# Seven block products instead of eight in the down-projections of six units of an MLP

## The reference, cut to what matters

```python
attn_out = jnp.einsum('btT,bTd->btd', attn, v) @ Wp + bp
cms_out = jax.nn.gelu(attn_out @ cW1 + cb1, approximate=False) @ cW2 + cb2
cms_out = cms_out + target_embed
concat = jnp.concatenate([attn_out, cms_out], axis=-1)
modifier = jax.nn.gelu(concat @ mW1 + mb1, approximate=False) @ mW2 + mb2
out = jnp.clip(x + cms_out + modifier, 0.0, 1.0)
```

## Time and profile before

| | us |
|---|---|
| median of 3 runs | 2095.6 (2093.02 to 2096.95) |
| the profiled execution | 2094.39 |
| its span, first to last instruction | 2092.6 |
| TensorE busy | 2077.7, 9644 matmuls |
| VectorE busy | 1313.0 |
| ScalarE busy | 922.0 |
| GpSimd busy | 274.2 |

### The profile page before, as it was taken

One profiled execution on the slowest core, in us unless ns is written; L12 is line 12 of the kernel. 1 busy time (PEld: TensorE's weight loads), 2 busy tenths in 40 slices (PEclk: granted clock), 3 DMA queues, 4 the chain that ended last, 5 costly groups with the idle time before them and its releaser, 6 DMA issues.

```text
span 2092.6 us, 26680 instructions
## 1 busy us (share of the span) xinstructions
PE 2077.7 (99%) x9644; PEld 1719.5 (82%) x9644; DVE 1313.0 (63%) x2089; ACT 922.0 (44%) x1604; POOL 274.2 (13%) x282
## 2 busy tenths in 40 slices
PE   8999999999999999999999999999999999999998
PEld 7888888888788888888888888888878888888886
DVE  6576675546767667455677667555476766754557
ACT  5464443333356444333335544443334645433342
POOL 0011112210101102112000110112100111121101
PEclk9999999999999999999999999999999999999999
DMA  7411211122321121221460112111342011112233
GB/s 283 162 31 41 71 66 51 61 71 97 141 81 41 51 86 36 71 70 47 164 205 31 51 51 76 61 48 66 110 145 92 21 51 55 62 61 71 71 106 91
DMA packets 42367, 169.70 MB, mean 81 GB/s; under 512 B 5624, under 2 KB 9720, under 8 KB 34808
## 3 DMA queue, kind: packets, MB, share of 16 engines
q1 hardware_dynamic: 42096, 167.97, 23.6%
q10 hardware_dynamic: 144, 0.03, 0.0%
HBM read 146.97 MB, written 21.01 MB: 80 GB/s over the span
## 4 chain that ended last, share of the span: by engine, by line
PE 95%; DVE 2%; ACT 1%; issue 1%; DMA 0%; SPq 0%; ACTq 0%; DVEq 0%
PE psum L579 86%; PE psum L871 2%; PE psum L834 2%; PE psum L654 1%; PE psum L676 1%; PE psum L874 1%; PE psum L847 1%; DVE acc L1447 0%; DVE fpart L1217 0%; PE psum L859 0%; PE psum L837 0%; ACT wup L1112 0%; PE psum L677 0%; PE psum L656 0%; DMA fraw<-fuse_in 0%
## 5 line engine op out<-in xcount | busy, mean ns | idle before, releaser
L579 PE MATMUL psum<-hs,wd 128*128 128x512 f32 x3072 | 717.9, 389 | 1.8 <-DVE acc L1447 1.8
L579 PEld LDWEIGHTS psum<-hs,wd 128*128 128x128 f32 x3072 | 576.0, 188 | 123.5 <-DVE acc L1447 3.5
L1447 DVE TENSOR_TENSOR acc<-psum,acc 128x512 f32<-128x512 f32 x448 | 294.5, 685 | 175.5 <-PE psum L579 174.3
L579 PE MATMUL psum<-cop,wsm 128*128 128x512 f32 x1416 | 354.7, 389 | 0.0
L579 PE MATMUL psum<-aop,wsm 128*128 128x512 f32 x1320 | 333.0, 389 | 0.0
L579 PE MATMUL psum<-aop,wsc 128*128 128x512 f32 x1320 | 311.3, 389 | 0.0
L579 PEld LDWEIGHTS psum<-cop,wsm 128*128 128x128 f32 x1416 | 265.8, 188 | 55.1
L579 PEld LDWEIGHTS psum<-aop,wsm 128*128 128x128 f32 x1320 | 247.8, 188 | 51.4
L579 PEld LDWEIGHTS psum<-aop,wsc 128*128 128x128 f32 x1320 | 247.5, 188 | 51.4
L1074 ACT ACTIVATE hs<-psum,bias 128x512 fp32r<-128x512 f32 x144 | 98.2, 682 | 394.5 <-PE psum L579 394.5
L1217 DVE TENSOR_TENSOR hs<-zt,hs 128x512 fp32r<-128x512 f32 x256 | 181.0, 707 | 125.6 <-ACT zt L1075 125.6
(11 more groups left out here) (167 smaller groups left out, 2214.6 us busy)
## 6 DMA issues: line engine op xcount, KB each, us to landing
w1m<-m_in SPq DMA_DIRECT2D x32, 1024.0 KB, 4.9
w1c<-c_in SPq DMA_DIRECT2D x32, 512.0 KB, 3.5
w<-c_in SPq DMA_DIRECT2D x32, 512.0 KB, 3.5
w<-m_in SPq DMA_DIRECT2D x32, 512.0 KB, 3.5
gains<-roles_in SPq DMA_DIRECT2D x30, 512.0 KB, 4.7
fw<-fused SPq DMA_DIRECT2D x6, 2048.0 KB, 10.0
fused<-fw SPq DMA_DIRECT2D x4, 2048.0 KB, 7.5
xmid<-x SPq DMA_DIRECT2D x4, 2048.0 KB, 6.4
```

The source lines that it names most:

```text
L579: mm = nc.tensor.matmul(out, lhs(a), rhs(b), start=(start and n == 0), stop=(stop and n == total - 1), skip_group_check=reopened)
L1447: nc.vector.tensor_tensor(dst, d_out[o][:, :], dst, ALU.add).then_inc(acc_done, 1)
```

## The change

In units 9 to 14 of each pass (`FAST`) the down-projection becomes a 2x2 block multiplication with seven products too. The blocks are: output halves of 256 features, hidden blocks of 128, token halves of 512. A down product has two outputs of three matmuls, 42 matmuls a unit.

- **TensorE.** `fast_down` puts each down product between two hidden products of the next unit: P1, D5, P5, D3, P6, D1, P2, D6, P7, D7, D2, P4, D4, P3 (D for down product). The products accumulate in two pairs of banks: D5 opens `d_a` and D3 adds to it; D1 opens `d_a` again and is copied to `d_b` (`copy_down`, ScalarE), D2 adds to `d_a`, and D6, D7, D4 to `d_b`. D3 waits for VectorE's `fast_add` of D5, D1 for that of D3, D7 for that of D6, D4 for that of D7.
- **VectorE.** Six `fast_add` of 128x1024 take the place of eight adds of 128x512. Three hidden operands and one more (H10 becomes an operand of a sum only) need `hidden_sum` (four differences of hidden blocks) and `low_sum` (four low parts). `low_part` splits seven weight operands of 128x256, `down_part` goes. The order is written out in `second_unit`.
- **ScalarE.** `split_part` (seven, 128x256), `split_sum` (four), `copy_down` (128x1024), one gelu less; an order of its own in `second_unit`.
- **GpSimd.** `combine_down` forms four sums of 128x256 of the second weights, after `combine` of the same unit; the first waits for w2 and for the last low part of the unit before, the fourth for the low part of D5's weights.
- **Storage.** The seven slots of the first weights become a ring of four, the second weights get a ring of five. The raw hidden values are written where the low parts go, no longer to `zt`, and several waits on low parts become waits on the gelu. The loads of w2 wait for the last `low_part` of the unit before, which now comes in the middle of the unit.
- **Unit 15.** It keeps the old down-projection, with the adapter's preparation in another order. `BY_POOL`, which was 0, goes with its dead branches.

```diff
+FAST = range(NG + 1, UNITS - 1)
+DOWN = (P5, P3, P1, P6, P7, P2, P4)
+SPLIT = (P5, P7, P6, P4)
+W1_SLOTS, W2_SLOTS = 4, 5
...
+            def combine_down(p, u):
+                f = fasts(p, u)
+                pool.wait_ge(w2_loaded, 16 * (UNITS * p + u + 1))
+                if u == FAST[0]:
+                    pool.wait_ge(prod[P3], strassen(p, NG))
+                else:
+                    pool.wait_ge(d_lo, d_at(p, u))
+                nc.gpsimd.tensor_tensor(comb2[:, 0, :], w2_block(2, 1), w2_block(2, 2), ALU.add).then_inc(w2_sums, 1)
+                pool.wait_ge(w2_sums, 4 * f + 1)
+                nc.gpsimd.tensor_tensor(comb2[:, 1, :], comb2[:, 0, :], w2_block(1, 1), ALU.subtract).then_inc(w2_sums, 1)
+                nc.gpsimd.tensor_tensor(w2_block(2, 1), w2_block(1, 1), w2_block(2, 1), ALU.subtract).then_inc(w2_sums, 1)
+                pool.wait_ge(d_lo, d_at(p, u) + 1)
+                pool.wait_ge(w2_sums, 4 * f + 2)
+                nc.gpsimd.tensor_tensor(comb2[:, 0, :], w2_block(1, 2), comb2[:, 1, :], ALU.subtract).then_inc(w2_sums, 1)
...
                     for u in range(UNITS):
                         if not plain(u):
                             combine(p, u)
+                        if fast(u):
+                            combine_down(p, u)
...
+            def fast_down(p, u, *which):
+
+                n, f, a0 = UNITS * p + u, fasts(p, u), acc_at(p, u)
+                for i in which:
+                    pe.wait_ge(d_lo, d_at(p, u) + DOWN.index(i) + 1)
+                    if i in SPLIT:
+                        pe.wait_ge(ht_lo, 4 * f + SPLIT.index(i) + 1)
+                    else:
+                        pe.wait_ge(h_lo[{P1: H11, P2: H01, P3: H00}[i]], n + 1)
+                    if i in (P6, P2):
+                        pe.wait_ge(d_copied, f + 1)
+                    else:
+                        pe.wait_ge(acc_done, {P5: a0 - (1 if fast(u - 1) else 2), P3: a0 + 1, P1: a0 + 2, P7: a0 + 3, P4: a0 + 4}[i])
+                    out = d_b if i in (P6, P7, P4) else d_a
+                    first = i in (P5, P1)
+                    for o in range(2):
+                        mm = product(out[:, o, :], [(lambda a: part(u, i)[:, a, o * P:(o + 1) * P], lambda c: h_operand(i, c), None)],
+                                     first, True, not first)
+                    mm.then_inc(dn_done, 1)
...
+                    if fast(u - 1):
+                        terms(p, u, P1)
+                        fast_down(p, u - 1, P5)
+                        terms(p, u, P5)
+                        fast_down(p, u - 1, P3)
+                        terms(p, u, P6)
+                        fast_down(p, u - 1, P1)
+                        terms(p, u, P2)
+                        fast_down(p, u - 1, P6)
+                        terms(p, u, P7)
+                        fast_down(p, u - 1, P7, P2)
+                        terms(p, u, P4)
+                        fast_down(p, u - 1, P4)
+                        terms(p, u, P3)
...
+            def second_unit(p, layer, u):
+
+                then = fast(u - 1)
+                if then:
+                    make_z12(p, u - 1)
+                    weight_part(p, u, P2)
+                    hidden(p, u - 1, H00)
+                    low_sum(p, u - 1, P7)
+                    hidden_sum(p, u - 1, P4)
+                    fast_add(p, u - 1, P5)
+                    low_sum(p, u - 1, P6)
+                    weight_part(p, u, P7)
+                    hidden(p, u - 1, H01)
+                    low_part(p, u - 1, P2)
+                    low_sum(p, u - 1, P4)
+                    fast_add(p, u - 1, P3)
+                weight_part(p, u, P4)
+                if then:
+                    low_part(p, u - 1, P4)
+                weight_part(p, u, P3)
+                if then:
+                    fast_add(p, u - 1, P6)
+                else:
+                    add(p, layer, u - 1, 0, *range(KC))
+                if fast(u):
+                    low_part(p, u, P5, P3)
+                    make_z22(p, u)
+                    weight_part(p, u + 1, P1)
+                    if then:
+                        fast_add(p, u - 1, P7)
+                        fast_add(p, u - 1, P2)
                     else:
+                        add(p, layer, u - 1, 1, *range(KC))
+                    weight_part(p, u + 1, P5)
+                    low_part(p, u, P1, P6)
+                    hidden_sum(p, u, P5)
+                    hidden_sum(p, u, P6)
+                    hidden_sum(p, u, P7)
+                    weight_part(p, u + 1, P6)
+                    low_sum(p, u, P5)
+                    hidden(p, u, H11)
+                    if then:
+                        fast_add(p, u - 1, P4)
+                    add_x(p, layer, u)
+                    low_part(p, u, P7)
...
```

More of the change, by code:

```diff
@@ L1422, in hidden, with low_part, hidden_sum, low_sum @@
                 dve.wait_ge(h_hi[h], UNITS * p + u + 1)
-                minus(hs[:, b, LO, m, :], h_raw(h), hs[:, b, HI, m, :]).then_inc(h_lo[h], 1)
+                if fast(u):
+                    dve.wait_ge(ht_made, 4 * fasts(p, u) + {H11: 1, H00: 3, H01: 4}[h])
+                minus(hs[:, b, LO, m, :], h_raw(u, h), hs[:, b, HI, m, :]).then_inc(h_lo[h], 1)
+            def low_part(p, u, *which):
+                for i in which:
+                    dve.wait_ge(d_hi, d_at(p, u) + DOWN.index(i) + 1)
+                    minus(part(u, i)[:, LO, :], part_source(i), part(u, i)[:, HI, :]).then_inc(d_lo, 1)
+            def hidden_sum(p, u, i):
+                n, f = UNITS * p + u, fasts(p, u)
+                if i == P5:
+                    dve.wait_ge(h_hi[H10], n + 1)
+                    dve.wait_ge(h_hi[H11], n + 1)
+                elif i == P6:
+                    dve.wait_ge(h_hi[H00], n + 1)
+                    dve.wait_ge(ht_made, 4 * f + 1)
+                elif i == P4:
+                    dve.wait_ge(h_hi[H01], n + 1)
+                    dve.wait_ge(dn_done, dn_at(p, u))
+                    dve.wait_ge(ht_made, 4 * f + 2)
+                left = {P5: h_raw(u, H10), P6: h_raw(u, H00), P7: h_raw(u, H00), P4: h_raw(u, H01)}[i]
+                right = {P5: h_raw(u, H11), P6: h_sum(P5), P7: h_raw(u, H10), P4: h_sum(P6)}[i]
+                nc.vector.tensor_tensor(h_sum(i), left, right, ALU.subtract).then_inc(ht_made, 1)
+            def low_sum(p, u, i):
+                f = fasts(p, u)
+                dve.wait_ge(ht_hi, 4 * f + SPLIT.index(i) + 1)
+                dve.wait_ge(ht_made, 4 * f + {P5: 2, P7: 3, P6: 4, P4: 4}[i])
+                minus(h_operand(i, LO), h_sum(i), h_operand(i, HI)).then_inc(ht_lo, 1)
+            def fast_add(p, u, i):
+                half, b, bank = {P5: (1, 0, d_a), P3: (0, 0, d_a), P6: (0, 0, d_b), P7: (1, 0, d_b), P2: (0, 1, d_a), P4: (1, 1, d_b)}[i]
+                dve.wait_ge(xadd_done, NG * p + u - NG + 1)
+                dve.wait_ge(dn_done, dn_at(p, u) + DOWN.index(i) + 1)
+                dst = x_block(half, b)
+                nc.vector.tensor_tensor(dst, bank, dst, ALU.add).then_inc(acc_done, 1)
             def make_z22(p, u):
```

323 lines of the change are left out of this document (215 added, 108 removed).

## The result

The changed kernel takes 2146.1 us (median of four runs, 2135.3 to 2148.0) against 2095.0 (2093.0 to 2097.0): ratio 1.0235, interval 1.0204 to 1.0266. The forecast was 2127, at most 2142. The profiled execution of the changed kernel is its fastest, 2135.3 us with a mean clock of 0.994; the others have 0.988 to 0.990. So the trace accounts for 40.9 us over the profiled execution of before, and the median holds 11 more that it doesn't show.

What follows compares the result with a forecast made beforehand. TensorE, busy 99% of the span, was taken to bound the kernel. From 2094.4 us, 34.1 saved by removed matmuls and pass ends, plus 66.8 of stalls before D3, gave 2127 us, 1.5% slower; range 2098 to 2142.

Steps and rivals of the forecast that it cites:

- The matmuls: Down-projection on TensorE: six fewer in 6 units and 4 passes, 144 x 0.2267 = 32.6 us saved, 9,500 left.
- the end of the pass: TensorE's wait for the last unit's first add shrinks from 0.76 to 0.26 + 0.13: 1.5 us less in four passes.
- The place of the wait: TensorE: about 24 idle stretches before D3, released by VectorE's add, 3 us each in 20, 65 us in all.
- The price of a collision: A 512 GpSimd sum asked for inside a dense row of VectorE's SBUF operations costs VectorE 1.10 us.
- Unit 9: First fast unit, with no fast_add P4 before it: a stall of 1.66 us before D3.
- The 1024 adds: VectorE's fast_add from PSUM, taken at 1.22 us each, bounds 1.19 and 1.37; the skill's count gives 1.19.
- I take no mutual delay: SyncE's w1 load, 1.5 us behind w2's, was still taken to land 4.9 us after issue.
- the first collision: GpSimd's first sum of the next unit, begun once w1 landed, delays VectorE's low_part P3 by 0.75 us.
- rival (a): Only two collisions, if w1 lands about 1.5 us later: stall 2.34 us, 2114 us in total; chance 0.18.
- the stalls before D3: TensorE waiting for fast_add P5 in the fast units: 4 x (5 x 3.01 + 1.66) = 66.8 us.
- A stall of 3.01 us a unit: D3 starts at 31.57 instead of 28.56 us in the unit's cycle, against 1.36 saved; repeats as a period of 31.57.
- Rival (d): TensorE hides all, 2060 us; needs VectorE ahead everywhere, which the predicted operation order excludes; given no chance of its own.

Runs made afterwards that it cites:

- the reordered kernel: Changed kernel with VectorE's and ScalarE's whole order rewritten, no operation changed, left out or added: 2060.5 us, ratio 0.9835.
- the narrow sums: Changed kernel with GpSimd's sums of weights cut to 8 columns in units 9 to 15: 2078.7 us, ratio 0.992.
- the late sum: Changed kernel with GpSimd's P3 sum of the first weights also waiting for fast_add P5: 2113.1 us, ratio 1.0083.
- the filler: Changed kernel with eight matmuls (five in unit 9) into an unread PSUM bank just ahead of D3's wait: 2128.0 us, ratio 1.0161.
- the first reordered kernel: Changed kernel with VectorE's order alone edited, fast_add P5 behind hidden H00 and fast_add P3 moved up: 2122.4 us, ratio 1.0137.

## Why the prediction was wrong

The direction was right, and the sum lacked one term, the clock.

**Right, step by step.** The matmuls: 9,500, and 2060.5 in the reordered kernel shows that 34.1 us is what their removal and the end of the pass are worth. The place of the wait: 24 times before D3, for fast_add P5. The cause: VectorE's queue between the gelu of P4 and fast_add P5, lengthened by GpSimd's sums; the narrow sums and the late sum show it. The price of a collision: 1.10 forecast, 1.09 measured. Unit 9: 1.5 us, restart included, against 1.66. The 1024 adds: 1.214 on average against 1.22. The Trainium skill ("VectorE: DVE Perf Modes", TRN2 errata) has 120 + N cycles from PSUM, by which I had estimated 1.19; the row that I took is nearer.

**Off in size.** "I take no mutual delay" for w1 behind w2: w1's landing is 5.7 to 7.0 us after its issue in the units without a fall at their start, against 4.9, and the first collision is missing in 9 of 20 units. That is between the forecast and rival (a), whose condition (1.5 us later) was met in part of them. Without the slow matmuls the stalls before D3 sum to 62.3 us against 66.8.

**Missed, small.** Unit 15's z22. VectorE there has the adapter's first weights (the low part of wdn) ahead of z22, and that operation waits, through ScalarE, for a load:

```profile
507.33 1.23 DVE L1407 TENSOR_TENSOR wdn<-raw_d,wdn 128x1024 fp32r<-128x1024 f32 x1 [1.88 <-ACT wdn L1261]
508.48 0.68 DVE L1658 TENSOR_TENSOR zt<-psum,zt 128x512 f32<-128x512 f32 x1
```

2.1 us of idle time in three passes, 2.9 with the restarts.

**The step that failed.** "A stall of 3.01 us a unit ... Everything after it hangs on it, so it repeats": I priced a wait at its own length and 0.13 for the matmuls behind it, from a wait of 0.47 us, the only one of this kind before. No term, rival or bound had the clock: the cost of the matmuls behind a wait was put at 0.13 us, and behind seven of the 24 waits it was 1.6 us more, 11.4 us in the profiled execution.

The trace of before had a sign of it that I passed over. At its start TensorE is idle for 2.94 us, and in the 4 us behind that its granted clock is 0.63. The row from TensorE's timeline, and the window with the same columns as the earlier trace rows:

```profile
32.16 8.21 PE L579 MATMUL psum<-fpart 128*128 128x512 f32 x29 [2.94 <-DVE fw L1217]
```
```profile
32.10:36.10 4.00, 3.94 (x12) 3.18 (x12) 4.00 (x5) 2.81 (x5) 0.00 (x0) 0.63 0.46 128
```

The profiled execution of the changed kernel has its wait of 3.08 us there too, but no fall, and is 1.4 us ahead when both have issued 600 matmuls (126.2 against 127.6 us). With that the account closes: 2094.4 - 34.1 + 62.3 + 11.4 + 2.9 - 1.4 = 2135.5, and 2135.3 was measured. The clock's term alone would have made the forecast 2138.5; the other errors together take 3.2 off that.

For the median's further 11 us there is no trace. The mean clock of those executions speaks for more falls: at the lower level half of the time is lost, so 0.001 of the mean clock over 2133 us is 2.1 us; from 0.994 to 0.9893 that is 10. Thirteen or fourteen falls instead of seven would give it, as an estimate. That the 12 to 18 us above 2128 belong to idle TensorE is shown by the filler; the number of falls in an execution that wasn't traced is argued, all the more as one execution of the filler kernel had a mean clock of 0.948 at no cost. Why one wait of 2.75 us brings a fall and the next doesn't stays open.

**Rival (d)** (2060 us) had got nothing, since "the order above excludes it". The statement was true of that order, and the order was not a property of the change: the same operations in another one reach it.

## What to carry to other kernels

When an accumulation is fused (D3 onto D5's banks), write down the queue that stands between the last product's arrival and the add that it needs, and put into that queue what GpSimd will start on account of it: here GpSimd's eight sums a unit, wide or narrow, decided between 2.4% slower and 0.8% faster, while VectorE's load at 86% was harmless once the order was right. Moving one operation moves the wait to the next reader: three of these kernels had a period of about 31.1 us, with the wait at D3, at P4, or at D4 and D3, and only when the load of w2, its sums and the adds all had slack did the time fall. And a wait of TensorE of the lengths seen here (1.9 to 3.3 us) should be priced with the 1.6 us that may be lost behind it, and with what a fall moves: here it moved a load, and the load brought a collision.

## What the hardware showed that I had not expected

- TensorE came back from idle stretches of 1.86 to 3.27 us in the second MLP at its lower clock in some cases, for two groups of six matmuls (4.41 us instead of 2.80), and at its full clock in others, after up to 3.12 us idle. The stretch of about 3 us at the kernel's start had a fall behind it in the trace of before and none in that of the changed kernel.
- Keeping it at work for 1.98 us of the wait was enough that none of the falls came behind it.
- 1 MB of weights, issued 1.5 us behind 0.5 MB, landed 5.7 to 7.0 us after its issue; issued 2.7 to 3.2 us behind, 4.8 to 5.0. Issued only 0.6 us behind, in the first reordered kernel, it took 5.5 to 5.6 in pass 0, so the landing doesn't simply grow as the two come closer.
